# Two decoder layers with top-2 experts: row maxima subtracted by a 65th contraction row, with the operand laid out by on-chip transfers

## What is computed

```python
    scores = jnp.einsum('bhsr,bhlr->bhsl', q_r, k_r)
    attn = jax.nn.softmax(scores, axis=-1)
    ctx_c = jnp.einsum('bhsl,bld->bhsd', attn, kv_rope)
...
    x = x + jnp.tanh(g_xattn[1]) * _L1_xattn_ref(_layernorm(x, axis=-1), ctx_512, L1_xattn_Wq, ...)
    x = x + jnp.tanh(g_ffn[1]) * _L1_ffn_ref(_layernorm(x, axis=-1), L1_ffn_Wr, L1_ffn_Wg, L1_ffn_Wu, L1_ffn_Wd)
```

## Time and profile before

| what | value |
|---|---|
| median of 3 runs | 505.62 us (505.1 to 515.1) |
| profiled execution, its own time | 506.92 us |
| its span, first to last instruction | 505.1 us |
| mean granted TensorE clock | 0.945 of full speed |
| busy: PE, vector, scalar, GpSimd | 429.9, 329.0, 245.8, 135.1 us |

### The profile page before, as it was taken

How to read it: one execution, slowest core, us unless ns; L and a number is a source line. 1 busy time by engine, 2 the same in 40 slices (tenths; PEclk the granted TensorE clock), 3 DMA queues, 4 the chain that set the end, 5 groups by cost and what they waited for, 6 DMA issues and landing times. The chain is left out here.

```text
span 505.1 us, 8174 instructions
## 1 busy us (share of the span) xinstructions
PE 429.9 (85%) x2827; PEld 346.6 (69%) x2827; DVE 329.0 (65%) x778; ACT 245.8 (49%) x542; POOL 135.1 (27%) x138
## 2 busy tenths in 40 slices
PE   1676999768789988899988899788889789999996
PEld 0343444436569877799777797678788668778885
DVE  0889277653889656998459994669532247555884
ACT  1122587533459647388455695542345154444332
POOL 5715000002601116202046011335027760000640
PEclk9998899896779999999999999998989799999998
DMA  6993500017000000000000000014023452211230
GB/s 162 315 348 90 79 1 1 0 52 245 0 2 1 2 1 1 1 2 0 1 2 1 0 2 1 2 62 126 0 64 95 132 184 86 90 55 53 83 106 21
DMA packets 27768, 31.19 MB, mean 62 GB/s; under 512 B 5104, under 2 KB 25120, under 8 KB 27472
## 3 DMA queue, kind: packets, MB, share of 16 engines
q1 hardware_dynamic: 23328, 23.92, 14.7%
q0 software_dynamic: 4400, 6.75, 6.0%
HBM read 25.68 MB, written 7.60 MB: 66 GB/s over the span
## 5 line engine op out<-in xcount | busy, mean ns | idle before, releaser
L1650 DVE RECIPROCAL egh<-egh 128x256 bf16<-128x256 bf16 x44 | 76.7, 1743 | 7.4 <-ACT egh L845 7.4
L1288 PE MATMUL bank<-kv,probs 128*128 128x65 f32 x512 | 64.7, 270 | 2.1 <-DVE ctxn L1758 1.9
L1288 PEld LDWEIGHTS bank<-kv,probs 128*128 128x128 f32 x512 | 62.8, 193 | 2.8 <-ACT probs L925 1.7
L925 ACT ACTIVATE probs<-bank 128x512 f32<-128x512 f32 x64 | 37.4, 590 | 26.5 <-PE bank L1271 25.9
L1731 DVE TENSOR_REDUCE negm<-bank 128x2 f32<-128x512 f32 x64 | 41.4, 686 | 3.9 <-PE bank L1245 3.7
L1245 PE MATMUL bank<-Kh,Qs 128*128 128x256 f32 x128 | 32.7, 351 | 11.8 <-DVE negm L1731 5.6
L841 ACT ACTIVATE gu_all<-bank 128x512 bf16<-128x512 f32 x44 | 26.1, 593 | 33.6 <-PE bank L1083 33.6
L1267 PE MATMUL bank<-Qs,Kh 128*128 128x256 f32 x128 | 41.7, 326 | 0.0
L669 POOL TENSOR_SCALAR veps<-mv 128x2 f32<-128x2 f32 x12 | 2.7, 225 | 142.8 <-DVE mv L1482 142.8
L1271 PE MATMUL bank<-negmT,ident_r 128*128 128x256 f32 x128 | 36.6, 286 | 3.6 <-ACT negmT L915 3.6
L680 POOL TENSOR_TENSOR W<-w_in,W 128x512 fp32r<-128x512 f32 x24 | 30.0, 1281 | 34.8 <-issue 28.0
(11 more groups left out here) (212 smaller groups left out, 947.1 us busy)
## 6 DMA issues: line engine op xcount, KB each, us to landing
xs<-f3A SPq DMA_DIRECT2D x1, 2432.0 KB, 9.8
xin<-xs SPq DMA_DIRECT2D x19, 128.0 KB, 2.3
ys<-y SPq DMA_DIRECT2D x19, 128.0 KB, 2.0
...
w_in<-in_L_ffn_Wg SPq DMA_DIRECT2D x8, 256.0 KB, 3.5
w_in<-in_L_ffn_Wu SPq DMA_DIRECT2D x8, 256.0 KB, 2.8
w_in<-in_L_ffn_Wd SPq DMA_DIRECT2D x8, 256.0 KB, 3.0
```

The costliest lines, as they stand in the source:

```text
L925: done(act.activation(flat(pT[:, n % 3]), bank1(b, FILL_ST + h)[:], ACT.Exp), "p_ready")
L1288: ins = pe.matmul(bank_v(b, h // 2)[:, at:at + DC + 1], pT[:, n % 3, lt, t * P:(t + 1) * P], kv[:, b * T + lt], start=(lt == 0), stop=(lt ...
L1650: done(dve.reciprocal(eg[:, j], eg[:, j]), "e1")
```

## The change

The third matmul of each `scores_T` step goes. The second now multiplies 65 rows: rows 0 to 63 are the trailing keys with the leading queries, and row 64 is ones in `Kl` against the negated maxima in a new operand `Qm`. (The product of trailing keys with trailing queries is dropped.) `Qm` lies in partitions 0 to 64 for all heads, in two groups of four heads in turn, so the leading queries have to change partitions and the maxima have to go from eight partitions into one: both are done by DMAs on SP's queue. For each group n of four heads, `queries_in` issues two DMAs of 64 partitions by 512 numbers (128 KB each) and `maxima_in` one DMA of 4 by 256 numbers (4 KB): 12 per sequence, 48 in all. PE waits for them before heads 0, 4, 8 and 12 (`qm_loaded`).

The maxima are turned in two groups of eight heads: the first after the maxima's score of head 9, the second after `scores_T(1)`; the scalar engine copies each (8 partitions by 256), the second just before the exponential of head 1. `Qm` shares its space with `xin` and `xT` of the tiles, so the first `load_x` waits for the last `scores_T` too. SP's order in the last sequence is: weight loads 4 to 6, queries of groups 0 and 1, weight loads 7 to 12, maxima of groups 0 and 1, queries and maxima of group 2, weight loads 13 to 15, those of group 3, the rest. The vector engine's `Kl` is written once instead of twice per half, two small set-up activations become one over a single partition, and the constant `perm_c` gets a buffer of its own.

```diff
...
@@ -228,7 +227,7 @@
         Kh = sb("Kh", [P, B * S], F32R)
         Kl = sb("Kl", [P, B * S], F32R)
         negm = sb("negm", [P, T, NH])
-        negmT = sb("negmT", [P, S], F32R)
+        negmT = sb("negmT", [NH // 2, S], F32R)
         f_d = sb("fold_d", [P, T * H])
         rden = sb("rden", [P, 2, 2, T])
@@ -285,9 +284,11 @@
         NWIN = 4
         w_in = sb("w_in", [P, NWIN, IC * H])
+
         NXIN = 4
-        xin = sb("xin", [P, NXIN, H])
-        xT = sb("xT", [P, 2, 2, HC * P], F32R)
+        Qm = sb("Qm", [P, 8, S], F32R)
+        xin = Qm[:, 0:NXIN].bitcast(F32)
+        xT = Qm[:, NXIN:8].rearrange("p (n a) s -> p n a s", n=2)
         layer1 = ExitStack()
...
@@ -484,6 +486,21 @@
         def bank_v(b, pr):
             return bank[(7, 4)[pr % 2 if b < B - 1 else 0]]
+
+        def qm_at(h):
+
+            return 4 * (h // 4 % 2) + 2 * (h % 2) + h // 2 % 2
+
+        def max_at(h):
+
+            return 8 * (h // 8) + qm_at(h)
+
+
+        QM_LOADS = 3
+
+        def qm_loaded(eng, g):
+
+            eng.wait_ge(ld_qm[g % 2], 16 * QM_LOADS * (g // 2 + 1))
         def bank_s0(b):
...
@@ -602,11 +619,30 @@
                 sp.dma_start(w_in[:, k % NWIN].rearrange("p (c i) -> p c i", c=IC),
                              d[("L1_ffn_Wg", "L1_ffn_Wu", "L1_ffn_Wd")[m]][e].rearrange("(c p) i -> p c i", p=P)).then_inc(ld_w1[k % NWIN], 16)
+            def queries_in(b, n):
+
+                sp.wait_ge(S_["q_hi"], 8 * b + 2 * (n + 1))
+                if n >= 2:
+                    sp.wait_ge(S_["sT_ready"], NH * b + 4 * (n - 1))
+                elif b:
+                    sp.wait_ge(S_["sT_ready"], NH * b)
+                for par in range(2):
+                    at = 4 * (n % 2) + 2 * par
+                    sp.dma_start(Qm[0:DC, at:at + 2].bitcast(F32),
+                                 Qs[DC * par:DC * par + DC, par, 2 * n:2 * n + 2].bitcast(F32)).then_inc(ld_qm[n % 2], 16)
+
+            def maxima_in(b, n):
+
+                sp.wait_ge(S_["mT_sb"], 2 * b + n // 2 + 1)
+                at = 4 * (n % 2)
+                sp.dma_start(Qm[DC:DC + 1, at:at + 4].bitcast(F32), negmT[at:at + 4, None, :].bitcast(F32)).then_inc(ld_qm[n % 2], 16)
+
             def load_x(i):
                 if i == 0:
-                    sp.wait_ge(S_["perm_set"], 1)
+                    sp.wait_ge(S_["perm_set"], 2)
                     sp.wait_ge(scattered, 16 * 2 * T * NS)
+                    sp.wait_ge(S_["sT_ready"], NH * B)
                 if i >= NXIN:
                     sp.wait_ge(S_["xT_ready"], i - NXIN + 1)
                 sp.dma_start(xin[:, i % NXIN], xs[i * P:(i + 1) * P, :]).then_inc(ld_xin[i % NXIN], 16)
@@ -616,7 +652,31 @@
                 sp.wait_ge(S_["y_sb"], i + 1)
                 sp.dma_start(ys[i * P:(i + 1) * P, :], y[:, i % 2]).then_inc(y_out[i % 2], 16)
-            for k in range(18):
+            for k in range(NWIN):
+                load_w1(k)
+            for b in range(B - 1):
+                for n in range(2):
+                    queries_in(b, n)
+                for n in range(2):
+                    maxima_in(b, n)
+                for n in range(2, 4):
+                    queries_in(b, n)
+                    maxima_in(b, n)
+            for k in range(NWIN, 7):
+                load_w1(k)
+            for n in range(2):
+                queries_in(B - 1, n)
+            for k in range(7, 13):
+                load_w1(k)
+            for n in range(2):
+                maxima_in(B - 1, n)
+            queries_in(B - 1, 2)
+            maxima_in(B - 1, 2)
+            for k in range(13, 16):
+                load_w1(k)
+            queries_in(B - 1, 3)
+            maxima_in(B - 1, 3)
+            for k in range(16, 18):
                 load_w1(k)
             for i in range(NXIN):
                 load_x(i)
@@ -763,7 +823,8 @@
                     done(pool.memset(zero, 0.0), "zero_set")
                 if n == len(LN_ORDER) - 2:
                     loaded(pool, "sort")
-                    done(pool.tensor_copy(perm_c[:], xin[:, 0].rearrange("p (a s) -> p a s", a=2)), "perm_set")
+                    done(pool.tensor_copy(perm_c[:, 0], perm_in[:]), "perm_set")
+                    done(pool.memset(perm_c[:, 1], 1.0), "perm_set")
                     for e in range(3):
                         w1_split(e)
                 if n == len(LN_ORDER) - 1:
@@ -799,9 +860,7 @@
                         done(act.activation(ex[:, b % 2, t], sc[b % 2][:, t], ACT.Exp, bias=small[:, b % 2, 0, t:t + 1],
                                             accum_out=small[:, b % 2, 1, t:t + 1]), "exp0")
                     yield
-                done(act.activation(ident_r[:], ident[:], ACT.Copy), "act_const")
-                done(act.activation(negmT[:].rearrange("p (h k) -> p h k", h=2), ident[:, 0:2, None].to_broadcast([P, 2, P]), ACT.Copy),
-                     "act_const")
+                done(act.activation(Kl[DC:DC + 1, :], ident[DC:DC + 1, DC:DC + 1].to_broadcast([1, B * S]), ACT.Copy), "act_const")
                 yield
             def ffn0(b):
@@ -899,6 +958,15 @@
                     act.wait_ge(S_["q_ready"], 4 * b)
                 done(act.activation(f2s[:, 0], bank1(b, 0)[:], ACT.Copy), "f2_hi")
                 yield
+
+                def copy_max(g):
+
+                    act.wait_ge(S_["mT_ready"], 2 * b + g + 1)
+                    for n in range(2):
+                        if b or g:
+                            qm_loaded(act, 4 * b + 2 * (g - 1) + n)
+                    done(act.activation(negmT[:], bank[7][0:NP, g * S:(g + 1) * S], ACT.Copy), "mT_sb")
+
                 for n in range(4):
                     act.wait_ge(S_["q_ready"], 4 * b + n + 1)
                     if b >= 1 and n == 0:
@@ -909,10 +977,10 @@
                     if b < B - 1:
                         done(act.activation(wait_full(act, b, n), bank1(b, FILL_Q + n)[:], ACT.Copy), "q_full")
                     yield
-                for _ in range(NP):
-                    yield
-                act.wait_ge(S_["mT_ready"], b + 1)
-                done(act.activation(negmT[0:NH, :], bank[7][0:NH, 0:S], ACT.Copy), "mT_sb")
+                for k in range(NP):
+                    if k == NP // 2:
+                        copy_max(0)
+                    yield
                 yield
                 if b == 0:
                     act.wait_ge(S_["f_fold"], NP)
@@ -922,6 +990,8 @@
                         act.wait_ge(S_["sT_ready"], n + 1)
                         if n >= 3:
                             act.wait_ge(S_["pv_ready"], n - 2)
+                        if h == 1:
+                            copy_max(1)
                         done(act.activation(flat(pT[:, n % 3]), bank1(b, FILL_ST + h)[:], ACT.Exp), "p_ready")
                     if h >= 7 and (h - 7) % 4 == 0:
                         k = (h - 7) // 4
...
@@ -1194,7 +1264,7 @@
                     elif n == 1:
                         pe.wait_ge(S_["m_lo"], NP)
                     elif n == 2:
-                        pe.wait_ge(S_["k_split"], 4)
+                        pe.wait_ge(S_["k_split"], 2)
                     elif n == 3:
                         pe.wait_ge(S_["g_lo"], 1)
                     for j in range(2):
@@ -1237,6 +1307,15 @@
                     done(ins, "q_ready")
                     yield
+                def turn_max(g):
+
+                    pe.wait_ge(S_["m_ready"], NH * b + NP * (g + 1))
+                    if b and g == 0:
+                        pe.wait_ge(S_["ctx_ready"], NP * b)
+                    for t in range(T):
+                        ins = pe.transpose(bank[7][0:NP, g * S + t * P:g * S + (t + 1) * P], negm[:, t, g * NP:(g + 1) * NP], ident[:])
+                    done(ins, "mT_ready")
+
                 for h in range(NH):
                     par, pr = h % 2, h // 2
                     bk = wait_fill1(pe, b, FILL_S + h)
@@ -1245,30 +1324,25 @@
                         ins = pe.matmul(bk[:, t * S:(t + 1) * S], Qs[:, par, pr, t * P:(t + 1) * P], Kh[:, kb],
                                         start=True, stop=True)
                     done(ins, "s_ready")
+                    if h == NP + 1:
+                        turn_max(0)
                     if b:
                         output(b - 1, h // NP, h % NP)
                     if h % 2:
                         yield
-                pe.wait_ge(S_["m_ready"], NH * (b + 1))
-                if b:
-                    pe.wait_ge(S_["ctx_ready"], NP * b)
-                for t in range(T):
-                    ins = pe.transpose(bank[7][0:NH, t * P:(t + 1) * P], negm[:, t], ident[:])
-                done(ins, "mT_ready")
                 yield
                 def scores_T(h):
                     par, pr = h % 2, h // 2
                     bk = wait_fill1(pe, b, FILL_ST + h)
+                    if h % 4 == 0:
+                        qm_loaded(pe, 4 * b + h // 4)
                     for t in range(T):
```

(18 more changed lines are left out.)

11 lines of the change are left out of this document (6 added, 5 removed).

## The result

The changed kernel takes 520.95 us (median of four runs, 519.66 to 522.52), against 505.67 for the kernel before (505.1 to 515.1). The ratio is 1.0265, with a 95% interval of 1.0197 to 1.0332: 13 to 15 us slower where 6.6 us faster was forecast. (Ratios leave out executions more than 1.5% above the fastest of the same kernel.) The interval's lower end lies just under 2%; the repeat in experiment 11 has 1.0224 there. The profiled execution took 522.11 us (before 506.92), its span is 520.2 (505.1), its mean granted clock 0.888 (0.945).

A forecast was written before the change was run, and what follows sets the result against it. PE, vector and scalar engines were taken as nearly full together, the vector engine ending the shared stretches. Gains of 7.0 us less 0.4 in the last sequence made 6.6, from 505.62 to 499.0 us; range 495.0 to 504.0.

The forecast's parts named there:

- I expect a fall, worth half of the 3.0 to 3.5 us at the low level: 1.5: Last sequence, after PE's 4.4 us wait: the granted clock falls to 1.2 GHz for a short time, costing 1.5 us.
- The clock falls in the shared stretches: Rival: small PE waits there lower the clock once per sequence, 1.5 us each, giving 503.5 us; chance 0.10.
- the shared stretch: From the maxima's turn to the first down product, three engines nearly full; forecast gain 1.2 us each in sequences 1 and 2.
- the 4.8: Sequences 0 to 2, up to the first down product: gains of 2.4 + 1.2 + 1.2 us, bounded by the vector engine.
- 7.0 forecast up to the last sequence: Set-up and sequences 0 to 2: total gain of 4.8 + 1.9 + 0.3 = 7.0 us.
- 1.87: Sign: PE's head with a gate step takes 1.87 us, the scalar engine's pace, not PE's own 1.75.
- no wait of PE for a DMA in sequences 0 to 2: Sign: the new query and maxima transfers stay hidden in sequences 0 to 2 and cost nothing.
- the rival of late copies: Rival: on-chip copies land late in every sequence, a loss from about 6 us landing, 510.5 us at 7; chance 0.12.
- The last sequence's stall: Last sequence: PE waits 4 to 4.5 us for `Qm`, its maxima transfers queued behind weight load 12 and GpSimd's splits.
- The last sequence without the stall: Rival: maxima land in 1.7 us and the clock holds, 2.3 us gained there, 496.3 us; chance 0.20.
- the 2.5 forecast: Last sequence: first values in effect 2.5 us late, 1.0 from the wait and 1.5 from the clock's fall.
- 2.15 us of gain: Last sequence, after the first values: heads 2 to 4 gain 0.7 us and heads 7 to 15 about 1.45.

The follow-up runs named there:

- experiment 11: Two kernels: 128-row second product, early maxima transfers, late f3A transposes and first product made twice, 502.65 us (0.9919); and the changed kernel repeated, 518.61 to 528.04 us (1.0269).
- experiment 3: Changed kernel with the second product over 128 rows (rows 65 to 127 zeros) instead of 65: 507.07 us, ratio 1.0001.
- experiment 1: Changed kernel with the last sequence's two maxima transfers issued before weight load 10 instead of behind load 12: 519.6 us, ratio 1.0267.
- experiment 5: Changed kernel with both the 128-row second product and the last sequence's early maxima transfers: 509.84 us, ratio 1.0059.
- 10: Changed kernel, 65 rows kept, with early maxima transfers and the last sequence's f3A transposes after two more heads: 513.09 us, ratio 1.0101, two runs.
- 8: Changed kernel with 128-row second product, early maxima transfers, and the last sequence's f3A transposes and copy after two more heads: 504.31 us, ratio 0.9933.
- 4: Changed kernel with the first product of each head and half made twice in the last sequence: 513.55 and 523.45 us.
- 6: Changed kernel with early maxima transfers and the 128-row second product in the last sequence alone, 65 rows in the others: 510.1 us, ratio 1.0048.
- experiment 9: Changed kernel with 128-row second product, early maxima transfers, and the first product made twice in the last sequence: 503.79 us, ratio 0.9914.

## Why the prediction was wrong

The rows of the second product carry most of the loss, in three pairs that differ in nothing else but the zeros written for them: 1.0265 and 1.0001 (changed kernel, experiment 3), 1.0267 and 1.0059 (1, 5), 1.0101 and 0.9933 (10, 8). That is 13, 10 and 8.5 us for 65 rows instead of 128 (the last from two runs). In the traces of experiments 1 and 5 the first values start at 355.09 and 354.82 and the last transposes at 400.45 and 390.86, so nearly all of it arises in the last sequence's heads.

**The step that failed** is "I expect a fall, worth half of the 3.0 to 3.5 us at the low level: 1.5". The fall was right. Its price was read from the earlier trace rows, where the clock comes back within four microseconds, and in that stretch PE streams three products of 128 rows for each half head. The change takes one away and cuts another to 65 rows. So the row was measured on a stream that no longer exists: what brings the clock back had been treated as a property of the stall. In its place the runs show a low stretch of 54 us, and a price of 13 us: that much comes back when the product's rows alone are put back (1.0265 to 1.0001), though the wait and the fall stay. A rival of this kind was missing. "The clock falls in the shared stretches" carried the same price of 1.5, and it came true as well. After the wait of 3 us for the last gate of sequence 2 the clock falls in the trace of the result (0.50 from 302 to 304 us, where the kernel before has 1.00) and in all ten traces of its variants and its repeat. After the same wait in sequence 1 it falls in five of the eleven: those of experiments 4, 6 and 8 and both of 11. There it costs 2.8 us (6, 8) and 5.9 and 5.8 us (4 and the repeat), by the time to the next first down product. The argument against it, that PE stays busy 19.3 of 22.8 us, overlooked that what PE saves is gathered in one wait at the end.

In the trace of the result PE is busy 18.00 of 18.00 us from 375 to 393 and stays at 1.2 GHz all the while. The Trainium skill, page "TensorE: Matmul & The Clock Gate", section "What's actually happening", says that the gate opens once PE has been busy for a sustained while; here the measurement decides: after 18 us in which the profile shows PE busy, the clock had not risen.

**Sequences 0 to 2**: from one first down product to the next, 0.7 behind the shared stretch and 1.2 in it were forecast, together 1.9; 1.6 was measured, for sequence 1 and for sequence 2. That the stretch ends with the vector engine, the base of the 4.8, was right: it idles 0.24 us in sequence 1, and PE waits 2.98 for it. But the total is nearly right by luck, for its parts aren't. From the end of the vector engine's last maximum to that of its last gate product the kernel before takes 237.28 - 213.47 = 23.81 us in sequence 1 and the changed one 234.43 - 211.25 = 23.18: 0.6 gained and not 1.2, and 0.9 comes from ahead of it. The reason shows in the order of time, here of the kernel before and then of the changed one:

```profile
236.86 0.42 DVE L1644 TENSOR_TENSOR egh<-egh,gu_all 128x256 bf16<-128x256 bf16 x2
...
238.03 1.28 POOL L731 TENSOR_TENSOR ctxs<-fold_d,ctxs 128x512 fp32r<-128x512 f32 x1 [6.28 <-ACT fold_d L933]
```

```profile
232.91 1.37 POOL L791 TENSOR_TENSOR ctxs<-fold_d,ctxs 128x512 fp32r<-128x512 f32 x1 [5.05 <-ACT fold_d L1003]
...
232.94 1.49 DVE L1722 TENSOR_TENSOR egh<-egh,gu_all 128x256 bf16<-128x256 bf16 x2
```

Since PE turns the contexts earlier, GpSimd's subtraction now runs beside the last two gate products, and these take 1.49 us instead of 0.42; in sequence 2 the same happens (299.63 and 299.65, 1.49 again). That is 1.07 us in each, right in front of PE's wait. No run moves the subtraction away, so that it is the cause is read from the overlap and not tested. The forecast hadn't asked what an earlier PE sets off on the other engines.

At the first down product of sequence 2 experiment 3's kernel is 305.82 - 298.50 = 7.3 us ahead (experiment 1's, with 65 rows, 7.4), against 7.0 forecast up to the last sequence; the changed kernel's execution was 4.4 ahead, having stood 2.1 us behind at 128 us, from a longer stretch of low clock at 49 to 58 us (0.50, against 0.66 and 1.00 before), ahead of anything that the change touches. A head with a gate step is 222.70 - 220.94 = 1.76 us long, not 1.87: the scalar engine doesn't take over; the vector engine alone sets the end. The second maxima's copy costs PE a wait of 0.99, which I had hidden under the first; it stands in a stretch that the vector engine bounds.

**The transfers**: no wait of PE for a DMA in sequences 0 to 2, as forecast, and the rival of late copies is out. The last sequence's stall has its forecast place, size (4.02 for 4.4) and cause. All engines of the changed kernel in order of time:

```profile
349.14 3.75 POOL L740 TENSOR_TENSOR W<-w_in,W 128x512 fp32r<-128x512 f32 x3 [6.25 <-issue]
...
352.92 0.37 SPq L619 DMA_DIRECT2D w_in<-in_L_ffn_Wg  x1
353.33 1.32 SPq L638 DMA_DIRECT2D Qm<-negmT  x2
```

The splits start at 349.14 (351.35 forecast), the maxima are issued at 353.33 (355.6), PE goes on at 356.22, 2.9 us after the first issue: the landing of 2.9 that I took from the weight load (358.5 - 355.6) holds. All of it is about 2 us early because the sequences ahead had gained, which the forecast's times of the kernel before don't include.

**The last sequence without the stall** was a rival at 496.3. Taking the stall away (experiment 1) brought nothing by itself: the wait for `f3A` took its place. I had used that wait only as something that hides the stall, and not asked what it does when PE comes early.

**The remaining gap.** With 128 rows the clock costs less and the kernel only ties (507.07 against 506.81). Of the 7.3 us in hand at 298.50, 5.8 are left at the last sequence's scores that wait for `Qs` (337.18 against 342.99), 2.7 at the first values (356.88 against 359.60), 2.9 at the last transposes (388.69 against 391.56) and 1.0 at the end. The second step is the stall, 3.1 us for the 2.5 forecast. In the third, 2.15 us of gain were forecast and 0.2 came, and the fall behind `ctxn` lasts 6 us with two products instead of under 4 with three, which fits. The first step holds two low stretches: the one behind sequence 2's wait (0.56 and 0.58 from 298 to 302 us) and one of 0.50 from 320 to 328. The last holds one of 0.66 from 400 to 405. No experiment isolates them.

What stays open: which measure of PE's stream the clock follows. Rows (three pairs), and the number of wide products (experiment 9) both move it. How soon it comes back with two products of 128 rows varies too: 3 and 6 us in experiment 3, 22 in experiment 5, and why is open. So is why one and the same wait of 3 us is followed by a fall in every trace in sequence 2 and in five of eleven in sequence 1.
